# Running a causal-attention kernel's row maxima 67 items ahead of the scores in place of 75

## The reference

```
x = x + attention(layernorm(x))     # 16 heads of 32 features, rotary positions, causal softmax
x = x + ffn(layernorm(x))           # 512x512 projection + bias, plus 8 LoRA experts of rank 16, top 2 by softmax
scores = where(causal, (q @ k.T) / sqrt(32), -inf);  attn = softmax(scores);  ctx = attn @ v
```

## Time and profile before

| | |
|---|---|
| median of 3 runs | 1598.35 us (1597.73 to 1603.5) |
| the profiled execution's own time | 1599.37 us |
| its span, first to last instruction | 1597.6 us |
| granted TensorE clock, mean over the span | 0.989 |
| TensorE busy (matmuls) | 1546.3 us, 97% |
| VectorE, GpSimd, ScalarE busy | 72%, 55%, 48% |

### The profile page before, as it was taken

One profiled execution on the slowest core, in us unless ns is written; L12 is line 12 of the kernel. 1 busy time (PEld: TensorE's weight loads), 2 busy tenths in 40 slices (PEclk: granted clock), 3 DMA queues, 4 the chain that ended last, 5 costly groups with the idle time before them and its releaser, 6 DMA issues. The chain is left out here.

```text
span 1597.6 us, 24861 instructions
## 1 busy us (share of the span) xinstructions
PE 1546.3 (97%) x9088; PEld 970.4 (61%) x9088; DVE 1146.8 (72%) x2273; ACT 767.1 (48%) x1539; POOL 884.3 (55%) x593
## 2 busy tenths in 40 slices
PE   6999999799999999999999999999999987999999
PEld 5888887545555555555555555555555436777777
DVE  6766666767777777777777777777777676666665
ACT  3222222144557566666666666665665663223221
POOL 2333323255787787787787787787787621112111
PEclk9999999988999999999999999999999999999999
DMA  5555785492376367368368358359444363222321
GB/s 198 204 204 178 233 282 172 139 211 54 81 156 156 86 139 174 81 134 184 81 133 185 81 121 197 80 113 196 89 100 126 87 139 106 80 79 80 128 83 53
DMA packets 120399, 215.83 MB, mean 135 GB/s; under 512 B 12502, under 2 KB 45782, under 8 KB 113110
## 3 DMA queue, kind: packets, MB, share of 16 engines
q1 hardware_dynamic: 102380, 136.20, 31.3%
q0 software_dynamic: 8064, 58.72, 18.2%
q10 hardware_dynamic: 9840, 19.40, 3.4%
HBM read 96.23 MB, written 58.72 MB: 97 GB/s over the span
## 5 line engine op out<-in xcount | busy, mean ns | idle before, releaser
L1040 ACT ACTIVATE a_probs<-a_st 128x512 f32<-128x512 f32 (+2 forms) x1244 | 583.6, 536 | 370.9 <-PE a_st L948 363.8
L239 DVE TENSOR_REDUCE a_part<-a_mx 128x1 f32<-128x512 f32 (+2 forms) x842 | 537.7, 681 | 114.4 <-PE a_mx L224 98.3
L903 POOL TENSOR_TENSOR a_pair<-a_probs 128x1024 f32<-128x1024 f32 (+2 forms) x224 | 398.0, 1803 | 38.9 <-ACT a_probs L1040 15.2
L224 PE MATMUL a_mx<-a_k_stack,a_q_stack 96*128 96x512 f32 (+3 forms) x640 | 243.4, 406 | 1.7 <-DVE a_part L239 0.4
L903 POOL TENSOR_TENSOR a_gather<-a_probs 128x1024 f32<-128x1024 f32 x76 | 179.6, 2385 | 104.2 <-ACT a_probs L1040 104.2
L224 PEld LDWEIGHTS a_mx<-a_k_stack,a_q_stack 96*128 96x128 f32 x640 | 117.6, 190 | 164.0 <-DVE a_part L239 121.1
L948 PE MATMUL a_st<-a_q_stack,a_k_stack 98*128 98x512 f32 (+2 forms) x604 | 210.2, 367 | 1.6 <-DMA a_q_stack<-a_neg_rows 1.6
L242 DVE CUSTOM_DVE_ANT_0 a_mx<-a_mx,f_ctx 128x384 f32<-128x384 f32 (+1 forms) x240 | 148.8, 632 | 86.6 <-PE a_mx L224 86.6
L357 POOL TENSOR_TENSOR p_rot<-p_mul 128x1024 f32<-128x1024 f32 x32 | 89.8, 2809 | 204.3 <-DVE p_mul L637 204.3
L1279 POOL TENSOR_TENSOR f_x<-f_x,f_bias 128x512 f32<-128x512 f32 x32 | 41.6, 1330 | 208.2 <-DVE f_xn L1493 208.2
L961 PE MATMUL a_av<-a_probs,shared 128*32 128x512 f32 (+3 forms) x1280 | 153.1, 551 | 0.0
(11 more groups left out here) (194 smaller groups left out, 2389.2 us busy)
## 6 DMA issues: line engine op xcount, KB each, us to landing
a_gather<-a_pair POOLq DMA_DIRECT2D x56, 1024.0 KB, 7.2
a_k_stack<-qk_scratch SPq DMA_DIRECT2D x72, 256.0 KB, 8.3
qk_scratch<-p_rot_hi SPq DMA_DIRECT2D x32, 512.0 KB, 3.1
qk_scratch<-p_rot_lo SPq DMA_DIRECT2D x32, 512.0 KB, 3.9
a_q_first<-qk_scratch SPq DMA_DIRECT2D x48, 256.0 KB, 6.8
a_q_stack<-qk_scratch SPq DMA_DIRECT2D x48, 256.0 KB, 4.9
v_scratch<-p_v_st SPq DMA_DIRECT2D x32, 256.0 KB, 7.6
ctx_scratch<-a_ctx_st SPq DMA_DIRECT2D x32, 256.0 KB, 2.7
```

The costliest lines, as they stand in the source:

```text
L224: mm = pe.matmul(places[:, i, :], queries[0:96, head, qi * P:(qi + 1) * P], keys[0:96, head, 0:width], start=(i == 0), stop=not masked_her ...
L239: dve.tensor_reduce(found, scores.rearrange("p (h n) -> p h n", n=width), AX.X, ALU.max).then_inc(self.max_done, 1)
L903: pool.tensor_tensor(place[:, h:h + 2, q0:TT], probs[:, s % RING, h:h + 2, q0:TT], probs[:, (s + 1) % RING, h:h + 2, q0:TT], ALU.add).then ...
L1040: act.activation(probs[:, s % RING, h, q0:TT], score_bank(g, HG * s + h)[:, q0:TT], ACT.Exp, scale=SCORE_SCALE).then_inc(exp_done, 1)
```

## The change

```diff
-HEAD_START = NITEM // 2 + 5
+HEAD_START = NITEM // 2 - 3
```

## The result

The changed kernel takes 1632.7 us (median of 4 runs, 1626.7 to 1642.9) against 1598.8 us of the kernel before (1597.7 to 1603.5): a ratio of 1.0217, with a 95% interval of 1.0174 to 1.026. The runs of the changed kernel differ by 16 us, those of before by 6. The profiled execution is the slowest of them, 1642.9 us, so its terms add up to more than the median's.

A forecast was written before the change was run, and what follows sets the result against it. `attend` was taken as bound by TensorE, busy 97% of the span. -3.7 + 23.5 + 4.1 + 10.2 = +34.1 us on the profiled 1599.4 gave 1633.5, less 1.0 to the median: 1632.4 us, range 1617 to 1652.

The forecast's parts named there:

- The place and its kind: Before unit 3's first score in every group: TensorE waits for the DMA into the query tile, 2 to 4 us.
- The path to the shift: Unit 3, pair 10 from 532.16: item 0's product at 537.05, its maximum 538.00, shift 539.57, issues 2.56 us.
- The landing: From the last issue of unit 3's shift to TensorE's release: 1.63 us, said to be rather high.
- The net cost in a group: Groups 0 to 6: first score of unit 3 4.05 us later, 0.7 back in pair 9, net 3.35 us.
- Group 0: Pair 5 with 7 items in place of 15 gives back 3.7 us, the only clear gain.
- Group 7: Pair 10's start to the release takes 10.47 us in place of 6.38: 4.1 us more.
- The clock: Falls to 1.2 GHz behind the waits, 1.7 us each in six of seven groups: 10.2 us.
- The rival without a fall of the clock: Unit 3's stall without any fall of the clock: +23.9 us, 1622 us; chance 0.22.
- the rival of the longer stall: Unit 3: issues take 3.83 us, or the clock stays low twice as long: 1643 to 1656 us; chance 0.22.
- What was to be free: Row paths of units 2, 0 and 1, about 6 us each, stay hidden behind pairs of some 6 us.

The follow-up runs named there:

- late75: The kernel before with unit 3's unit_max and shift one pair later, at pair 10, in groups 0 to 6: 1649.6 us (1.0327).
- pull67: The changed kernel with 9 items in each of pairs 6 to 9, so unit 3 ends in pair 9 again: 1602.9 us (1.0027).
- lead73: The kernel before with HEAD_START NITEM // 2 + 3 in place of + 5: 1636.5 us (1.0238).
- fill67: The changed kernel with nine unread 128x512 products on TensorE before unit 3's first score in groups 0 to 6: 1619.1 us (1.0114).
- again67: The changed kernel run once more, unaltered, for a second profile: 1640.2 us (1.0245).
- lead74: The kernel before with HEAD_START NITEM // 2 + 4 in place of + 5: 1593.8 us (0.9967).
- now67: The changed kernel with each unit's unit_max right behind its last item, not behind all items of the pair: 1610.4 us (1.0068).
- split75: The kernel before with PLAN[10] 140 in place of 141, so the next group's item 0 is first of pair 10: 1596.8 us (0.9981).

## Why the prediction was right, and where it wasn't

The time was met (1632.4 foretold, 1632.7 measured), but by two errors that cancel, which is luck: the wait was priced some 8 us too high and the clock some 7 too low. The mechanism was as foretold; its sizes were not.

- **The place and its kind: right.** TensorE waits for the four DMAs into the query tile before unit 3's first score in every group, and late75, pull67 and lead73 tie the loss to it.
- **The path to the shift: right to 0.1 us.** Item 0's product came 4.81 us after the start of pair 10 (537.05 - 532.16 = 4.89 foretold), its maximum 5.77 (5.84), the shift 7.34 (7.41). The four issues took 2.56 us in the absence of the accumulating DMA, as foretold. That this DMA makes them slower, and not traffic as such, agrees with two other places of the changed kernel. Unit 1's shift, at pair 16, stands behind such a DMA and took 4.03 us at 586.26. Unit 2's in group 3 went out beside 270 GB/s of loads, with the next such DMA issued only behind it, and took 2.56:

```profile
749.72 2.56 SPq L270 DMA_DIRECT2D a_q_stack<-a_neg_rows  x4
```
```profile
749.70:752.30 2.60, 2.60 (x16) 1.26 (x15) 2.00 (x4) 1.73 (x5) 2.50 (x2) 1.00 1.16 270
```

- **The landing: 1.19 us (543.86 to 545.05), not 1.63.** It was read where the accumulating DMA was in flight. So TensorE was idle for 2.25 us, not 2.7.
- **The net cost in a group: 2.25 us, not 3.35.** fill67 has no falls in these groups, and its first scores of unit 3 at 540.37 and 1040.21 stand four periods apart, 124.96 us each, where before group 1's shift of unit 3 stood at 532.49 and group 6's at 1145.99, five periods of 122.7 us. I took the delay of the first score (4.05) less 0.7 for pair 9. The delay was 3.54 us (545.05 - 533.96 = 11.09 against 539.71 - 532.16 = 7.55), and pair 9's second half took 2.63 us (531.33 to 533.96) in place of 3.57, 0.94 back; another 0.34 came back elsewhere in the period. What counted in the end was about the idle time alone.
- **Group 0: -3.7 us, right.** Its pair 5 took 6.27 us in place of 9.94. **Group 7: 3.6 us, not 4.1**, again by the landing: from the start of pair 10 to the release it took 9.97 us against 6.38. TensorE's timeline of the changed kernel, group 0's pair 5 and group 7's pair 10, first and last:

```profile
374.88 0.50 PE L224 MATMUL a_mx<-a_k_first,a_q_stack 96*128 96x512 f32 x1
...
381.15 0.50 PE L224 MATMUL a_mx<-a_k_first,a_q_stack 96*128 96x512 f32 x1
...
1303.75 0.50 PE L224 MATMUL a_mx<-a_k_stack,a_q_stack 96*128 96x512 f32 x1
...
1313.72 1.65 PE L948 MATMUL a_st<-a_q_stack,a_k_stack 98*128 98x512 f32 x3 [3.28 <-DMA a_q_stack<-a_neg_rows]
```

- **The clock: the term that failed, 10.2 us foretold and up to 30 measured** in the profiled execution, some 17 in the median: the 33.9 us less the other terms as measured, 7 x 2.25 + 3.6 - 3.7 + 1.2 = 16.9 us (the 1.2 are group 4's wait before unit 2, below). I took the one low stretch of the trace before, 3.4 us, for the size of a fall; here they last from 3.4 to 10.2 us. Behind unit 3's waits of groups 0 to 6 they are 10.2, 10.2, 3.4, 10.2, none, 3.4 and 6.8, together 44.2 us, half of which is 22. The rest of the 30 is the fall behind group 4's wait before unit 2 (6.8 us low), group 7's stretch, 6.8 us in place of 3.4, and `finish`, which has 13.6 us low in two stretches (the longer is shown) in place of 6.8:

```profile
893.40:900.20 6.80, 6.80 (x37) 3.20 (x39) 2.95 (x5) 3.84 (x7) 3.58 (x4) 0.50 0.25 47
...
1313.20:1320.00 6.80, 6.28 (x28) 3.13 (x32) 1.25 (x2) 4.50 (x9) 0.00 (x0) 0.50 0.50 155
1361.00:1371.20 10.20, 6.08 (x14) 4.79 (x15) 2.80 (x2) 1.91 (x1) 0.89 (x4) 0.50 0.51 151
```

  The rival without a fall of the clock is out, and the doubled stretch in the rival of the longer stall was nearer. A low clock cost 4.5 us in 10.2, not quite the half that I took. Why a stretch lasts 3.4 us one time and 10.2 the next stays open.
- **What was to be free:** nearly. In group 4 TensorE also waited for unit 2's rows, 1.15 us (0.46 in again67), with a fall behind it (none in again67):

```profile
873.87 6.50 SPq L825 DMA_DIRECT2D a_q_first<-qk_scratch  x3
880.40 0.77 SPq L829 DMA_DIRECT2D ctx_scratch<-a_ctx_st  x1
881.22 2.57 SPq L270 DMA_DIRECT2D a_q_stack<-a_neg_rows  x4
```
```profile
891.62 0.50 PE L948 MATMUL a_st<-a_q_stack,a_k_first 98*128 98x512 f32 x1 [1.15 <-DMA a_q_stack<-a_neg_rows]
```

  The transposed rows were there by 878.3, but SyncE was still issuing loads of queries (the first row) and a store, 2.9 us. The shift was issued by 883.8 and released TensorE only at 891.6. The loads of the next group's keys, values and queries had gone out on the same queue just before; that the small DMAs stood behind them is argued, not shown. I had called a path of about 6 us safe with three pairs to spare, and it took 13.5 us from the transpose at 878.10.

lead74 is the fastest version found: 1593.8 us, 0.33% under the kernel before.

## What to carry to other kernels

A lead between two pipelined phases is not a dial but a set of deadlines: find for each hand-over the slack between the arrival (here 1.8 us) and the first use, and what stands in front of the hand-over in its queue. Within the slack the lead was free here; one item beyond it cost 43 us. Send a hand-over off behind its last input, not behind the batch that the input happens to be in. Where TensorE must wait for a couple of microseconds, price the clock behind the wait as well as the wait, and look whether there is work to put into it; here even useless work paid.

## What the runs showed of the hardware

- Waits of 2.2 us and more before unit 3, in groups 0 to 6 of the changed kernel (twice), lead73 and late75, had a stretch at 1.2 GHz behind them in 27 of 28 cases; waits of 1.1 to 1.4 us (now67) in none of 7, and filled ones (fill67) in none of 7. The length of a wait doesn't settle it: waits for the same DMAs of 1.15 us (group 4 of the changed kernel) and 1.55 us (group 7 before) had a low stretch behind them, those of 1.11 us (pull67), 1.39 (lead74), 1.50 (split75) and 1.62 (late75) in group 7 had none. The stretches behind the 27 lasted 3.4 to 13.7 us, and the same program got other ones in another run. The Trainium skill, page "TensorE: Matmul & The Clock Gate", section "HAM oscillation — how this bites in real kernels", tells of a fall behind each wait in a kernel that waits for a DMA in each turn; the waits there are longer.
- Four 4 KB DMAs from SBUF to SBUF took SyncE 2.56 us to issue at unit 3 and unit 0 of the changed kernel (2.87 at unit 3 of group 6), also beside 270 GB/s of plain loads (749.72), and 3.8 to 4.4 us where GpSimd had issued an accumulating DMA some 1 to 3 us before (both kernels). In the changed kernel TensorE was released 1.19 us behind the last issue, in group 1 and in group 7.
